# Latent attention on one core: the score items of a block ordered by tile length instead of by head

## What is computed

```python
kv_c = x @ W_kvd + b_kvd
keys_c, values = heads(kv_c @ W_ku + b_ku, HD), heads(kv_c @ W_vu + b_vu, HD)
keys_r = _apply_rope(heads(kv_c @ W_kr + b_kr, RD))
q_c = x @ W_qd + b_qd
q = concatenate([heads(q_c @ W_qu + b_qu, HD), _apply_rope(heads(q_c @ W_qr + b_qr, RD))])
scores = einsum('bhqd,bhkd->bhqk', q, concatenate([keys_c, keys_r])) * scale
probs = softmax(where(causal, -1e9, scores))
ctx = einsum('bhqk,bhkd->bhqd', probs, values)
...
x = x + (ctx @ W_o + b_o) + (xn @ binarize_weight(weight).T + bias)
```

## Time and profile before

| | us |
|---|---|
| median of 3 runs (lowest, highest) | 1438.58 (1436.43, 1440.43) |
| the profiled execution | 1437.48 |
| its span, first to last instruction | 1435.7 |
| PE busy | 1394.3 (97%) |
| ACT busy | 1204.1 (84%) |
| DVE busy | 1152.8 (80%) |
| POOL busy | 998.3 (70%) |
| mean granted TensorE clock | 0.997 |

### The profile page before, as it was taken

The page is one execution under the profiler, slowest core; times in us unless marked ns, Lnnn a source line. Parts: engine busy times, 40 slices in busy tenths (PEclk is TensorE's granted clock), DMA queues, the critical chain, the costliest instruction groups (busy, mean ns, idle before and its releaser), DMA issues.

```text
span 1435.7 us, 27603 instructions
## 1 busy us (share of the span) xinstructions
PE 1394.3 (97%) x9786; PEld 1262.7 (88%) x9786; DVE 1152.8 (80%) x2708; ACT 1204.1 (84%) x2603; POOL 998.3 (70%) x573
## 2 busy tenths in 40 slices
PE   6979999999999999999999999999999999999997
PEld 4769999998898999988898999999889999999987
DVE  4858898886778888887677889888677888888887
ACT  4658888996888988898688988999778988888886
POOL 6986687777567867768765777777765777666750
PEclk9999999999999999999999999999999999999999
DMA  9842212212333222211333222221233322221100
GB/s 271 223 122 56 70 47 63 63 49 62 80 100 79 78 63 63 63 42 38 77 92 96 65 70 63 64 63 49 63 74 88 88 58 64 63 63 49 41 20 30
DMA packets 46957, 106.82 MB, mean 74 GB/s; under 512 B 9333, under 2 KB 17830, under 8 KB 46822
## 3 DMA queue, kind: packets, MB, share of 16 engines
q1 hardware_dynamic: 43360, 94.01, 25.7%
q0 software_dynamic: 3296, 11.01, 2.7%
q10 hardware_dynamic: 166, 0.03, 0.0%
HBM read 48.92 MB, written 9.96 MB: 41 GB/s over the span
## 4 chain that ended last, share of the span: by engine, by line
PE 81%; ACT 7%; DVE 4%; POOL 3%; DMA 2%; SPq 1%; issue 1%; DVEq 0%; POOLq 0%; ACTq 0%
PE turn L1503 16%; PE ring L1448 11%; PE u_ps L1521 8%; PE ring L1480 8%; PE ring L1479 8%; PE u_ps L1522 8%; PE ring L1478 8%; PE o_ps L1541 4%; PE o_ps L1542 4%; ACT probs L759 2%; PE ring L1461 2%; PE ring L1387 2%; DMA swapped<-k_rope 2%; PE ring L1393 1%; POOL k_rope L348 1%; ACT probs_hi L768 1%
## 5 line engine op out<-in xcount | busy, mean ns | idle before, releaser
L1039 DVE TENSOR_SCALAR_CACHE_REDUCE probs<-ring,c_t 128x1024 f32<-128x1024 f32 (+7 forms) x512 | 414.5, 811 | 100.0 <-PE ring L1480 95.4
L1049 DVE TENSOR_TENSOR probs_lo<-turn,probs_hi 128x512 fp32r<-128x512 f32 (+1 forms) x640 | 401.5, 631 | 69.1 <-ACT probs_hi L768 64.0
L768 ACT ACTIVATE probs_hi<-turn 128x512 fp32r<-128x512 f32 (+1 forms) x640 | 349.9, 550 | 110.0 <-PE turn L1503 103.6
L759 ACT ACTIVATE probs<-probs,row_min 128x1024 f32<-128x1024 f32 (+7 forms) x512 | 394.2, 771 | 11.7 <-DVE probs L1039 9.2
L1503 PE MATMUL turn<-ident,probs 128*128 128x128 f32 x2304 | 387.9, 275 | 6.5 <-ACT probs L759 4.2
L1521 PE MATMUL u_ps<-probs_hi,kv_nat 128*128 128x256 f32 x1152 | 313.4, 301 | 0.0
L1503 PEld LDWEIGHTS turn<-ident,probs 128*128 128x128 f32 x2304 | 282.8, 140 | 32.5 <-ACT probs L759 9.9
L1522 PE MATMUL u_ps<-probs_lo,kv_nat 128*128 128x256 f32 x1152 | 288.7, 280 | 0.0
L1478 PE MATMUL ring<-k_hi,q_hi 128*128 128x512 f32 (+3 forms) x768 | 275.8, 359 | 0.0
L1480 PE MATMUL ring<-k_hi,q_lo 128*128 128x512 f32 (+3 forms) x768 | 263.3, 343 | 0.0
L1479 PE MATMUL ring<-k_lo,q_hi 128*128 128x512 f32 (+3 forms) x768 | 262.5, 342 | 0.0
(11 more groups left out here) (218 smaller groups left out, 2573.9 us busy)
## 6 DMA issues: line engine op xcount, KB each, us to landing
swapped<-k_rope SPq DMA_DIRECT2D x128, 128.0 KB, 2.3
wv<-wv_scratch SPq DMA_DIRECT2D x62, 256.0 KB, 4.1
wp<-wp_scratch SPq DMA_DIRECT2D x62, 192.0 KB, 3.5
wp<-wp_scratch SPq DMA_DIRECT2D x31, 256.0 KB, 3.1
swapped<-q_y SPq DMA_DIRECT2D x62, 128.0 KB, 2.3
swapped<-q_x SPq DMA_DIRECT2D x62, 128.0 KB, 2.3
k_hi<-qb_kv_hi SPq DMA_DIRECT2D x16, 256.0 KB, 3.7
k_lo<-qb_kv_lo SPq DMA_DIRECT2D x16, 256.0 KB, 4.7
```

The costliest lines, as they stand in the source:

```text
L759: act.activation(p, p, ACT.Exp, scale=-1.0, bias=row_min[:, r:r + 1], accum_out=row_sum[:, g % 4, w, h:h + 1]).then_inc(exp_ready, 1)
L768: act.activation(probs_hi[:, r % 4, 0:width], turn[r % 2][:, 0:width], ACT.Identity).then_inc(turned_hi, 1)
L1039: dve.tensor_scalar(probs_of(g, w, h), ring[slot_of(entry)][:, KEY_COLUMN[qt]:KEY_COLUMN[qt] + keys], c_t[b % 2][:, qt, ds(pair * 2 + h, 1 ...
L1049: dve.tensor_tensor(probs_lo[:, r % 4, 0:width], turn[r % 2][:, 0:width], probs_hi[:, r % 4, 0:width].bitcast(F32), ALU.subtract).then_inc ...
```

## The change

The four items of a block are taken in another order. Before, x meant long tile of head 0, short of head 0, long of head 1, short of head 1. After, it means long of head 0, long of head 1, short of head 0, short of head 1. The lists of ACT and DVE are not touched: they name x, so the instruction at the place of x = 1 is now a long one and that of x = 2 a short one. In PE's list the second chunk of a long tile moves from x = 2 to x = 1, and the wait on head 1's keys and queries (`head_ready(g, 1)`) comes before the scores of x = 1. The long tile's transposes wait for two exponentials of the block instead of three; the short tile's for all four, as before.

```diff
@@ exponent (ACT), minimum (DVE), scores (PE)
-                h, w = divmod(x, 2)
+                w, h = divmod(x, 2)
@@ mask (PE)
-                qt, entry = LONG_SHORT[g % BLOCKS][x % 2], ("score", g, x)
+                qt, entry = LONG_SHORT[g % BLOCKS][x // 2], ("score", g, x)
@@ turn_group (PE)
-                    pe.wait_ge(exp_ready, g * SCORE_ITEMS + 3 + w)
+                    pe.wait_ge(exp_ready, g * SCORE_ITEMS + 2 * (w + 1))
@@ PE's sequence, n == 0
                     weigh_group(g - 1, 1)
+                    head_ready(g, 1)
                     scores(g, 1, 0)
+                    scores(g, 1, 1)
                     turn_group(g - 1, 3, (g, 2))
-                    head_ready(g, 1)
                     scores(g, 2, 0)
-                    scores(g, 2, 1)
                     turn_group(g - 1, 4)
```

## The result

| | us |
|---|---|
| before, median of 4 runs (lowest, highest) | 1437.51 (1436.28, 1440.43) |
| after, median of 4 runs | 1479.51 (1477.66, 1480.88) |
| ratio after / before, 95% interval | 1.0284 (1.0265 to 1.0304) |
| profiled execution of after, its span | 1477.66, 1475.8 |

A forecast was written before the change was run, and what follows sets the result against it. TensorE was taken as the bound, so only its waits could change. The terms 31.1 + 7.5 - 1.8 = 36.8 us on 1437.48 gave 1474.3 us, range 1457 to 1496 us.

The forecast's parts named there:

- The first block: Block n = 0 of each pair: group 3 ends 1.11 us later, delaying q_x and the mask; 28 x 1.11 = +31.1 us.
- the chain closed: First block, 27 pairs: end of group 3 on TensorE, seven steps on ACT, mask on TensorE, without slack.
- the last pair: Its first block has no q_x, only the wait at the transposes, priced like the others at about 1.1 us.
- The waits that run beside it: First block: long exponential delays u_hi, u_pair and group 3's subtraction; transposes +0.8 us, overlapping the 1.11 rather than adding.
- The second block: Second block of a pair: exponentials and minima change places with idle time around them; taken as 0.
- The third block: Block n = 2: later, longer item-1 minimum delays the subtraction TensorE's group 3 needs; 0.26 us in 29 blocks, +7.5 us.
- both terms: Third block: +0.38 us wait at group 3, less 0.12 from the long tile's easier wait for exponentials.
- The pair-6 third blocks: Three third blocks with next batch's linear layer: 0.92 us exponential wait falls by 0.6 each, -1.8 us.
- The fourth block: Fourth block: item 1's scores grow by 0.18 us; between 0 and 0.18 can reach TensorE, taken as 0.
- the waits on L1461 behind q_x and on L1503 behind probs_lo: Sign in the profile after: these TensorE waits grown to some 30 us together, where they were a few.
- The clock: Forecast: granted clock still 1.00. Rival: falls after new gaps, 1 us lost in 28 pairs, 1502 us; chance 0.03.

## Why the prediction was right

**The first block, 31.1 us forecast, 31.7 measured: right, and for its reason.** The step "group 3 ends 1.11 us later, ScalarE waits in order, q_x and the mask with it" shows in each row: idle time 2.97 for a forecast of 2.94, q_x gapless, the mask 0.05 behind. Before with only group 3 late reproduces it (+28.0), and the new order in the first block alone costs +29.5. That the sum comes so close is partly luck, since small misses cancel. The 27 plain pairs lost 28.8 us for 30.0 forecast: I had called the chain closed, but u_hi was held by the weighing 0.05 us longer than by group 3 (see the run with group 3 early), and that much of the 1.11 us was absorbed. The three pair-6 blocks lost 0.3 us each, where I had expected none, the very first block was 0.3 us shorter, and the last pair lost 2.2 us instead of 1.1, which is the clock, below.

**The waits that run beside it: right that they do not add, one of them not seen.** The transposes start 9.61 us into the block, 8.74 before: +0.87 for a forecast of 0.8. But 0.63 of this is there already at the outputs (8.90 us into the block, 8.27 before). I had not named them: the long exponential delays, through u_hi, ScalarE's half of their `u_pair` too. Taking that wait away gave 0.02 us a block.

**The second block: right,** -0.02 us.

**The third block, 7.5 us forecast, 8.3 measured.** A plain one is +0.25 for a forecast of 0.26, by the delayed low part, shown by putting that part first. In the pair of the earlier trace rows both terms are there: group 3 starts 4.80 us into the block where it was 4.42, the 0.38 of the forecast, and by the end of the block 0.14 of it is given back, for 0.12. With the low part first the block is only 0.04 us shorter than before and not 0.12, since the next mask waits a little for the minimum. Pairs 5 and 7 of the first three batches lost 0.4 to 0.5.

**The pair-6 third blocks: term mis-sized, -1.8 us forecast, 0.0 measured.** TensorE in such a block, after:

```profile
359.61 0.23 PE L1461 MATMUL ring<-mask_bf,ident_bf 128*128 128x128 bf16 x1 [0.80 <-DVE probs L1039]
...
364.80 0.23 PE L1461 MATMUL ring<-mask_bf,ident_bf 128*128 128x128 bf16 x1 [0.27 <-DVE x_sb L1001]
...
368.06 0.55 PE L1503 MATMUL turn<-ident,probs 128*128 128x128 f32 x3 [0.33 <-ACT probs L759]
```

The wait for the exponential fell from 0.92 us to 0.33, by the 0.6 that I had said. But the first mask waits 0.80 us for the long minimum (0.61 before), and the mask of item 3 waits 0.27 us for VectorE to take the linear layer out of the ring: a short item now stands between the two where a long one covered it. I had followed the exponentials there, and not the ring.

**The fourth block, 0 taken, 2.2 measured.** The median of 0.09 is inside the bounds of 0 to 0.18; in pair 6 of the first three batches it was 0.3.

Together 36.8 us forecast, 41.6 measured by block, 42.0 by the medians. The 4.8 us between the first two are these terms: 1.8 in pair 6, 2.2 in the fourth block, 0.6 and 0.8 in the first and third, less 0.6 in the second.

**What I had wrong without a price.** I said that the waits on L1461 behind q_x and on L1503 behind probs_lo would show as some 30 us. They show as 7.5 us at weight loads and 9.9 us at matmuls, since the lost 1.1 us a block are spread over the outputs, the transposes and the mask, and part of each is hidden in longer matmul records. And I saw one chain in the first block where there are two: with group 3 out of the way, the long minimum of item 1 still costs 0.71 us a pair. The number did not suffer, because the chain of group 3 is longer and covers it, and that is luck too, for I had not looked; anyone who had tried to mend the new order by my explanation alone would have got back a third of it.

**The clock.** It stayed at 1.00, the 2.4 GHz level, from 97.6 to 1432.2 us of the trace of after, through some 50 short waits more than before; over the whole span its mean was 0.996, and 0.997 before. The Trainium skill ("TensorE: Matmul & The Clock Gate", section "A second HAM failure mode: psum-queue depth-cycling") tells of a kernel whose short idles between groups of matmuls made the clock fall and rise; in the pairs that carry the sum they did not do so in this trace. In the last pair it did fall. There q_x's projection is missing from TensorE's list, the wait in front of the outputs is 2.71 us long (1.20 before), and behind it stands

```profile
1432.20:1435.70 3.50, 3.50 (x17) 3.22 (x16) 2.11 (x6) 1.66 (x5) 0.00 (x0) 0.51 0.00 0
```

which is the 1.2 GHz level. The kernel with the low part ahead of the minimum has the same first block and the same wait of 2.71 us, and behind it

```profile
1427.00:1431.00 4.00, 3.81 (x29) 3.36 (x30) 3.30 (x8) 2.08 (x6) 0.00 (x0) 1.00 0.00 0
```

Its last pair lost 1.26 us in the first block, near the 1.1 of the forecast; that of after lost 2.21. So about 1 us of the 42 is the clock. Two of the four runs of after had a mean of 0.993 and were some 3 us longer, which is a small part of the difference at most.

## What to carry to other kernels

When a hand-written order is changed, price the instruction that gets a bigger one in front of it, not the one that comes earlier: write down who waits for it, then the whole list of that engine up to the next gap of idle time, and then who waits at its end. Look for every chain that starts at the bigger instruction; the longest hides the others, and mending it brings back only the difference. A run without gaps can still have a second entry, a step that waits for something else too: here an earlier start gained nothing past it, while a later one arrived almost in full (1.07 of 1.11 us).

## What the runs showed of the hardware

A wait costs TensorE more than the idle time that the trace shows. In the kernel with group 3 first and the exponential late, 0.31 us of idleness stand before the projection, while the distance of the starts is 0.60 us; without the wait it is 0.12, although the matmul in front is recorded as 0.28 us long in both. So the wait cost 0.48 us, and the next start after it came 0.33 us on, where without a wait it was 0.27. Over a pair the same: 0.49 us of idleness in 40.00 us for 1.4 us of time. Distances of starts between two fixed points of the program measure such losses; busy time and the list of waits do not.

The same wait did not always do the same to the granted clock. In each of the 13 traces TensorE waits 0.86 to 0.94 us for a mask in the fourth block of pair 7, once in each of the first three batches. Behind 4 of these 39 waits the clock fell, some 2 us later, to 0.50 for 3.4 us (the 1.2 GHz level), and that block took 1.6 us more than the same one of the other batches: in the kernels with group 3 first (from 774.3 us), with the outputs moved (763.0), with the first block alone (1118.2) and with blocks 1 to 3 (413.9). Behind the other 35 it stayed at 1.00. A single trace can therefore carry such a loss by chance.
